# Banded attention before a mixture of experts: the value product without its wholly masked query columns

## The reference, cut to what matters

```python
attn = jnp.einsum('bqhmd,bkhd->bhmqk', q, k) * sm_scale
mask = (q_pos >= k_pos) & (q_pos < k_pos + SW)        # SW = 64
attn = jnp.where(mask, -jnp.inf, attn)
w = jax.nn.softmax(jnp.concatenate([attn, sink], axis=-1), axis=-1)[..., :-1]
out = jnp.einsum('bhmqk,bkhd->bqhmd', w, v)
```

## Time and profile before

| what | value |
|---|---|
| device time, median of 3 runs | 1071.03 us (1070.24 to 1071.81) |
| profiled execution, first to last instruction | 1063.8 us |
| busy on TensorE, of that span | 1032.3 us (97%) |
| busy on VectorE | 918.9 us (86%) |
| busy on ScalarE, GpSimd | 653.7 us, 663.4 us |
| value product (L1536), PE busy | 247.9 us in 8192 matmuls |
| score tiles (L1512), PE busy | 280.6 us in 1024 matmuls |

### The profile page before, as it was taken

How to read it: one execution, slowest core, us unless ns; L and a number is a source line. 1 busy time by engine, 2 the same in 40 slices (tenths; PEclk the granted TensorE clock), 3 DMA queues, 4 the chain that set the end, 5 groups by cost and what they waited for, 6 DMA issues and landing times.

```text
span 1063.8 us, 32339 instructions
## 1 busy us (share of the span) xinstructions
PE 1032.3 (97%) x13013; PEld 729.8 (69%) x13013; DVE 918.9 (86%) x1962; ACT 653.7 (61%) x1670; POOL 663.4 (62%) x607
## 2 busy tenths in 40 slices
PE   6899999999999999999999999999998999999996
PEld 4466666666666666666666666666566999999995
DVE  6999999999999999999999999999966777677773
ACT  4676667666667666667776656777654455544451
POOL 5657776767666888666777877667762422233332
PEclk8999999999999999999999999999999999999998
DMA  3544555544333344333343344333324344454421
GB/s 94 150 114 117 129 135 130 137 118 131 95 84 81 95 110 105 97 100 79 80 111 101 95 131 111 94 86 98 100 80 159 87 121 121 126 125 124 101 44 21
DMA packets 115574, 112.11 MB, mean 105 GB/s; under 512 B 35264, under 2 KB 103936, under 8 KB 115296
## 3 DMA queue, kind: packets, MB, share of 16 engines
q1 hardware_dynamic: 97648, 90.29, 31.3%
q0 software_dynamic: 7296, 8.55, 5.0%
q10 hardware_dynamic: 10480, 11.20, 3.8%
HBM read 74.84 MB, written 21.83 MB: 91 GB/s over the span
## 4 chain that ended last, share of the span: by engine, by line
PE 60%; DVE 35%; issue 2%; ACT 1%; DMA 0%; SPq 0%; POOLq 0%; DVEq 0%
PE bank L1536 21%; DVE probs_ring L1124 15%; DVE probs_t L1133 13%; PE bank L1701 11%; PE bank L1512 11%; PE bank L1712 7%; DVE heads_sb L1153 4%; PE bank L1715 4%; PE bank L1568 1%; PE bank L1441 1%; PE bank L1676 1%; PE bank L1458 1%; PE bank L1476 1%; PE bank L1596 1%; DVE neg_max L1124 0%
## 5 line engine op out<-in xcount | busy, mean ns | idle before, releaser
L841 ACT ACTIVATE probs_ring<-probs_ring,neg_max 128x512 f32<-128x512 f32 x512 | 365.9, 717 | 210.2 <-DVE neg_max L1124 209.4
L1124 DVE CUSTOM_DVE_ANT_0 probs_ring<-bank,mask,sink_neg 128x512 f32<-128x512 f32 x512 | 360.3, 738 | 24.9 <-PE bank L1512 23.8
L1133 DVE STREAM_TRANSPOSE probs_t<-probs_ring 128x1024 f32<-128x1024 f32 x256 | 317.8, 1241 | 0.2 <-ACT probs_ring L841 0.2
L1512 PE MATMUL bank<-qk_st 64*128 64x512 f32 x1024 | 280.6, 624 | 11.6 <-DVE neg_max L1124 7.4
L1536 PE MATMUL bank<-probs_t,v_quads 32*64 32x256 f32 x8192 | 247.9, 381 | 0.0
L1536 PEld LDWEIGHTS bank<-probs_t,v_quads 32*64 32x64 f32 x8192 | 179.3, 132 | 75.4 <-issue 48.1
L670 POOL TENSOR_TENSOR chunk_sb<-chunk_sb,rope_sb 128x512 f32<-128x512 f32 (+1 forms) x94 | 119.8, 1275 | 111.1 <-issue 80.6
L789 POOL DMA_INDIRECT out<-expert_sb,slots x40 | 77.8, 1945 | 150.6 <-DVE expert_sb L1385 143.3
L1512 PEld LDWEIGHTS bank<-qk_st 64*128 64x128 f32 x1024 | 85.3, 185 | 77.0 <-DVE neg_max L1124 41.5
L1043 ACT ACTIVATE hidden<-bank,b_sb 128x320 f32<-128x320 f32 x128 | 60.5, 524 | 107.1 <-PE bank L1701 107.1
L675 POOL TENSOR_TENSOR qk_st<-chunk_sb,swap_sb 128x512 f32<-128x512 f32 (+1 forms) x94 | 120.0, 1276 | 7.4
(11 more groups left out here) (189 smaller groups left out, 1352.5 us busy)
## 6 DMA issues: line engine op xcount, KB each, us to landing
v_quads<-v_rows SPq DMA_DIRECT2D x128, 128.0 KB
recip_wide<-recip_rows SPq DMA_DIRECT2D x64, 256.0 KB
w_raw<-in_L_ffn_w SPq DMA_DIRECT2D x14, 1024.0 KB, 8.2
swap_sb<-chunk_sb SPq DMA_DIRECT2D x314, 32.0 KB
w_raw<-in_L_attn_W_qkv SPq DMA_DIRECT2D x32, 256.0 KB, 2.9
slots<-slot_rows SPq DMA_DIRECT2D x9, 662.5 KB, 4.0
slot_rows<-x2T ACTq DMA_DIRECT2D x8, 662.5 KB, 6.2
w_raw<-in_L_attn_W_qkv SPq DMA_DIRECT2D x64, 64.0 KB, 2.7
```

Source lines behind the costliest of these rows:

```text
L841: nc.scalar.activation(probs[(g * UNITS + n) % RING][:, :], probs[(g * UNITS + n) % RING][:, :], ACT.Exp, bias=neg_max[j][:, n:n + 1], sca ...
L1124: nc.vector.tensor_tensor_reduce(probs[(g * UNITS + n) % RING][:, :], SCORE[SCORE_OF[n // 2][n % 2]][:, :], mask[:, L - P - t * P:2 * L - ...
L1133: nc.vector.transpose(probs_t[j][:, :, (h // 2) * (2 * P):(h // 2 + 1) * (2 * P)] .rearrange("p b (h q) -> p h b q", h=2)[:, :, :, t * BLK ...
L1512: nc.tensor.matmul(SCORE[SCORE_OF[n // 2][hh]][:, :], qk_st[j][half, h // 2, t * P:(t + 1) * P], qk_st[j][half, PAIRS, :], start=True, sto ...
```

## The change

For each key square, each quadrant now leaves out the one query tile (32 columns of each of the two heads of a pair) whose square lies wholly in the band. With `d` and `c` of the key square, that is tile `4*d + c + 1 - 4*a`, if it is 0 to 3. It exists for `d = a` with `c` = 0, 1, 2 (tiles 1, 2, 3) and for `d = a - 1` with `c` = 3 (tile 0; quadrant 0 has none). Where the tile left out is 1 or 2, the columns that remain are in two pieces, and the one matmul becomes two: 64 and 128 columns for `c = 0`, 128 and 64 for `c = 1`. Where it is 3 or 0, one matmul of 192 columns is left. Each quadrant takes its key squares in an order that starts from its own number, `d = (a + turn) % 4`, so that all four quadrants come to such a square in the same step. The order of the turns is 1, 0, 2, 3 for each `c`.

```diff
+            PV_ORDER = [(c, turn) for c in (0, 1, 2, 3) for turn in (1, 0, 2, 3)]
+
+            def value_step(j, c, turn, first, last):
+
+                for a in range(QUADS):
+                    d = (a + turn) % QUADS
+                    rows = slice(a * BLK, (a + 1) * BLK)
+                    hidden_tile = TPB * d + c + 1 - TPB * a
+                    tiles = [t for t in range(TPB) if t != hidden_tile]
+                    runs = [tiles[:hidden_tile], tiles[hidden_tile:]] if 0 < hidden_tile < TPB - 1 else [tiles]
+                    for p in range(PAIRS):
+                        out = PV[a][p * HD:(p + 1) * HD, 0:2 * P].rearrange("d (h q) -> d h q", h=2)
+                        seen = probs_t[j][rows, c * QUADS + d, p * 2 * P:(p + 1) * 2 * P].rearrange("k (h q) -> k h q", h=2)
+                        for run in runs:
+                            q = slice(run[0] * BLK, (run[-1] + 1) * BLK)
+                            ins = nc.tensor.matmul(out[:, :, q], v_quads[j][rows, d, c * HD:(c + 1) * HD], seen[:, :, q],
+                                                   start=first, stop=last)
+                return ins
...
-                    for blk in PV_AT[n]:
-                        c, d = divmod(blk, TPB)
-                        for a in range(QUADS):
-                            rows = slice(a * BLK, (a + 1) * BLK)
-                            for p in range(PAIRS):
-                                ins = nc.tensor.matmul(PV[a][p * HD:(p + 1) * HD, 0:2 * P],
-                                                       v_quads[j][rows, d, c * HD:(c + 1) * HD],
-                                                       probs_t[j][rows, blk, p * 2 * P:(p + 1) * 2 * P],
-                                                       start=(blk == 0), stop=(blk == BLOCKS - 1))
-                    if blk == BLOCKS - 1:
+                    for i in PV_AT[n]:
+                        ins = value_step(j, *PV_ORDER[i], first=(i == 0), last=(i == BLOCKS - 1))
+                    if i == BLOCKS - 1:
                         ins.then_inc(s_pv, 1)
```

## The result

The change made the kernel slower. In its first job the median was 1081.66 us of 5 runs (1077.33 to 1087.07) against 1071.03 us: a ratio of 1.011, 95% interval 1.0079 to 1.014. So it costs 12 to 13 us; 6.2 were forecast, and 1081.66 lies just above the range.

What follows compares the result with a forecast made beforehand. PE's three value-product bursts were taken to bound each group. Columns' savings and late-starting places summed to +0.17, +0.06 and -0.04, +0.19 us per group; 32 groups gave 1071.0 + 6.2 = 1077.2 us, range 1061 to 1081.5 (forecast's own 1074 to 1081).

Steps and rivals of the forecast that it cites:

- What bounds the kernel: PE's three value-product bursts (2.34, 2.34, 2.86 us) stand whole in each group's chain; DVE idles 0.42, 0.74, 0.51 us.
- The columns' term: In the value-product bursts, fewer columns save 0.10, 0.21 and 0.04 us: -0.35 us per group.
- The window: PE holds about 64 instructions, leaving in program order when finished; split steps start last places 0.27 us late in bursts one, two.
- The rival that the order costs nothing: In PE's bursts columns alone decide: -11.2 us, 1060 to 1063 us; chance 0.22.
- The reading from the five loads in time and three late ones: In a burst's third-step wave, loads six to eight straggle at 0.05 to 0.08 us, read as a window of about 64.
- The size per group: Value-product bursts change by +0.17, +0.06 and -0.04 us, +0.19 us per group; over 32 groups 6.2 us.
- without a pause: In burst one the late eighth place, starting at 0.80 us, then works through 0.33 + 3 x 0.43 us uninterrupted.
- The missing step: No fetch cost was forecast: the 64 added PE instructions per group were counted within +0.19 us, with no queue touched.
- the first rival: Order costs nothing in PE's bursts; stragglers have another cause, say instruction fetch: 1060 to 1063 us, chance 0.22.
- a fetch could not be late: Argument against fetch-caused stragglers in PE's bursts: instructions come at 4 to 5 ns and are used at 13.
- The fixed price per matmul: Rival: each PE matmul has an issue slot of about 27 ns; +15 to +22 us, 1086 to 1093 us, chance 0.05.
- 7.2 us above that span: The median was taken to stand 7.2 us above the profiled execution's 1063.8 us, giving the base of 1071.0 us.

Runs made afterwards that it cites:

- e3: The change without its split steps: only steps left with one 192-column piece are shortened, no instruction added; ratio 0.9961 against the kernel before.
- e6: The kernel before, only reordered: in bursts one and two each place does the second and third step's key squares in a row; ratio 1.0164.
- e4: The change with no column left out, but each matmul of the two split steps made as two of 128 columns; ratio 1.0193 against the kernel before.
- e1: The change with its split steps reordered: first pieces of all eight places, then second pieces; ratio 1.0051 against the kernel before.
- e2: The change's new order of key squares per quadrant alone, every matmul with all 256 columns; ratio 0.9994 against the kernel before.
- e7: The kernel of e3 once more, 12 runs: 1061.14 against 1064.46 us for the kernel before, ratio 0.9969.
- e8: The change unaltered, run again in a later job; ratio 1.0123 against the kernel before.
- e5: The change with 24 more small matmuls (96 instructions) at PE's start, to shift the instruction pieces' borders; ratio 1.0208.

## Why the prediction was right or wrong

**What bounds the kernel** was right: the bursts are on the path with their full length, gains (e3) and losses (e6) alike. DVE's idle times grew with the bursts' loss, from 0.42 to 0.45 us and from 0.74 to 0.89; the one before heads, which I had expected to grow too, stayed 0.51.

**The columns' term** was right in each size: a step of 192 columns brings 0.10 us (burst two of e3), the last step 0.04, and the quarter of the columns in a split step 0.10 (burst one of e4 against the change, 2.72 and 2.62).

**The window** was right as a mechanism, and it decided the sign. The rival that the order costs nothing would have given 1060 to 1063 us; it was undone by e1 and e6. The reading from the five loads in time and three late ones carried over to other bursts. Foretold were 2.50 and 2.39 for e1, 2.70 for both bursts of e4 and 2.69 for both of e6; measured were 2.50 and 2.39, 2.72 and 2.70, 2.72 and 2.71. That the leaving order is that of the program, and at the matmul's end, is the reading that fits all of them; I have no run that separates it from another rule with the same sums. The Trainium skill (TensorE: Matmul & The Clock Gate, the table at its head) gives the depth of 64; no run here varied it. In the changed kernel itself the start of the split step shows it (line L1513 in 441.68 to 441.74 us; the step begins at 441.69):

```profile
L1513 PE MATMUL bank<-probs_t,v_quads x13: 214/374/374, 441.5 to 441.7; 32*64 32x256 f32 x8, 32*64 32x64 f32 x5
```

Five places have begun with their 64 columns while eight matmuls of the step before still run. The records of the other three begin at 0.69, 0.73 and 0.76 us from the burst's start; e4 and e6 have the same three times. Such a record takes in the place's own weight load (it lasts 0.263 us, that of the first place 0.214), so the last place's columns begin at 0.81, where I had said 0.80.

One thing the window doesn't explain. In a whole step all eight places load their weights ahead, within 0.06 us, and so they do in e1. In the split step only the first place does, though the first loads of places two to four stand among the first 64 instructions. The loads (x) in the stretch where eight stood:

```profile
441.47:441.53 0.06, 0.06 (x1) 1.00 0.00 0
```

e6 has one there as well. So eight instructions in a row for one place also hold back the others' loads, by a rule that no run here shows. The times of the last places are met without it.

**The size per group** was a little short. The terms of bursts one and two, +0.17 and +0.06, measured +0.21 and +0.08; burst three's -0.04 was exact. 0.19 was said and 0.24 came, 1.4 us over the kernel. The start of the last place and its split step (0.33 us) were as forecast. The sum took it that the place then works "without a pause": in burst one its first matmul of the next step had its load in part before it (a record of 0.398 us instead of 0.374), 0.02 us. The rest is rounding, 0.43 for 0.431 and the like. Burst two was said at 2.48 and came at 2.49.

**The missing step** is the larger part, and the one that failed: that instructions have to be fetched. It stood at nothing in the sum. I wrote that the 64 more instructions of a group "are in that figure" and that "no DMA or queue is touched". The queue of instruction fetches is touched: 103 packets became 111, and burst one and burst two now have 192 instructions each, so that a piece border falls in each of the two in 20 of the 32 groups, where it did in 10. The fetches of the kernel before were on its page's list of queues, and the prediction read nothing from it. To this I put the 4 to 6 us by which the measured time exceeds the bursts' 7.5. I even used fetching against the first rival, "a fetch could not be late"; for the stragglers that held, and as a general sentence it was wrong.

**The fixed price per matmul** of 27 ns was rightly held unlikely: split steps took far less than 0.86 us.

**Left open.** The profiled execution of the change stood 21.5 us over the one before, where 10.6 lie between the medians; the one is some 5 us over its median and the other some 5 us under it, which the prediction's "7.2 us above that span" had hidden. By the last group 16.3 were lost: 7.5 by bursts, 8.2 by stalls, the rest in groups next to a fall of the clock, such as 6.8 us at 1.2 GHz from 783 us on, where the kernel before had 3.4. Another 5 us went in the first expert, with one wait there:

```profile
PE bank L1713 <- ACT hidden L1043: 2.8, 1, 2.8
```

Behind it stand 3.4 us at 1.2 GHz, from 847.8 us on, that the kernel before didn't have. The profiles of e2 and e3, which add nothing, have the same wait (2.7 and 3.0 us), the ones of before, e7 and e8 don't. So it belongs to single executions and not to the change.

Why a border stalls in one execution and not in the next was not tried, but the traces of the change and e8 show a part of it. Group 14 stalled in the change, where the fetch of the next piece began 3.08 us after PE's first matmul of the piece before, and not in e8, where it began after 1.89. Group 3 is the other way round, 2.09 and 3.29 us. From the fetch's start to the new piece's first matmul these four took 2.5 to 2.9 us. So a late start of the fetch goes with the stall, not a longer fetch; what delays the start stays open.

## What to carry to other kernels

Where many small matmuls run in separate places of the array, count instructions as well as columns: a place whose next instruction stands more than a window (some 64 instructions by the reading here) behind the oldest unfinished one waits, however free it is. Leave out columns where one matmul stays one matmul; a cut that makes two of it can cost more than it saves. And see how many PE instructions a dense stretch consumes in the time of one instruction fetch, 2.3 to 3.0 us from its start to the first matmul here, since a kernel can sit just at the edge of that, as the kernel before did.

## What the runs showed of the hardware that was not expected

- Order alone, with the same instructions and columns, moved a burst of 80 matmuls from 2.41 to 2.72 us (e6).
- PE's instruction fetches of 16 KB, 256 instructions, can be seen stopping it: all 21 stalls listed for the change, e5 and e8 were at the same place of a piece, 200 or 201 past a multiple of 256 in the program's count, each 0.5 to 2.1 us from matmul to matmul. Moving the program by 96 instructions moved all but the first to other groups (e5).
- Tiny matmuls are not free: 48 matmuls of 8 columns, each with a load of 128 columns, took 7.1 us at the kernel's start, 0.11 us each at 2.4 GHz and 0.21 at 1.2 GHz (e5).
- Eight instructions in a row for one place hold back the weight loads of the others: one load stood ahead where eight did with four in a row (the change and e6 against before and e1).
